# A decoder layer on one core: the cross-attention's masked maxima write their unread sum into the scores' own PSUM bank, not into the residual tile

## The reference

```python
x = _layernorm(x + _L0_attn_ref(x, ...), axis=-1)              # self-attention, 32 heads of 16, no mask
x = _layernorm(x + _L0_xattn_ref(x, ctx_1024, ctx_1024, 0, mask_SxS2_ff0), axis=-1)
x = _layernorm(x + _L0_ffn_ref(x, ...), axis=-1)               # routed, sign weights

# _L0_xattn_ref: 32 query heads, 8 key/value heads (4 query heads share one), head width 16
scores = jnp.einsum('bsgrd,btgd->bgrst', xq, xk) / math.sqrt(HEAD_DIM)
scores = scores + mask                                          # mask is [128 query tokens, 128 context tokens]
probs = jax.nn.softmax(scores.astype(jnp.float32), axis=-1)
out = jnp.einsum('bgrst,btgd->bsgrd', probs, xv)
```

## Time and profile before

| | us |
|---|---|
| median of 3 runs (lowest to highest) | 406.38 (402.18 to 407.63) |
| the profiled execution's own time | 409.41 |
| its span, first to last instruction | 407.6 |
| busy: PE, PEld | 341.6, 244.0 |
| busy: DVE | 267.6 |
| busy: ACT, POOL | 153.7, 113.0 |
| mean granted TensorE clock | 0.864 of full speed |

### The profile page before, as it was taken

How to read it: one execution, slowest core, us unless ns; L and a number is a source line. 1 busy time by engine, 2 the same in 40 slices (tenths; PEclk the granted TensorE clock), 3 DMA queues, 4 the chain that set the end, 5 groups by cost and what they waited for, 6 DMA issues and landing times.

```text
span 407.6 us, 7606 instructions
## 1 busy us (share of the span) xinstructions
PE 341.6 (84%) x2661; PEld 244.0 (60%) x2661; DVE 267.6 (66%) x974; ACT 153.7 (38%) x293; POOL 113.0 (28%) x203
## 2 busy tenths in 40 slices
PE   1693789997889999997999999879899965699563
PEld 1692556795647758975567499666556743444342
DVE  0968653558757648688785497878756777804444
ACT  3852135420144854302375733023755520046220
POOL 3362400131240314433422155421121431000321
PEclk9998568998895999996999999959999976579755
DMA  8948800167570001784510026955000155000001
GB/s 282 374 152 241 183 4 6 56 191 220 145 185 5 12 22 57 206 248 122 167 55 5 0 82 192 260 134 160 5 14 2 44 145 142 4 2 2 0 1 51
DMA packets 26703, 42.59 MB, mean 104 GB/s; under 512 B 8153, under 2 KB 18529, under 8 KB 24361
## 3 DMA queue, kind: packets, MB, share of 16 engines
q1 hardware_dynamic: 26393, 41.58, 36.1%
q10 hardware_dynamic: 272, 0.52, 0.3%
HBM read 29.32 MB, written 12.32 MB: 102 GB/s over the span
## 4 chain that ended last, share of the span: by engine, by line
PE 65%; DVE 20%; issue 5%; DMA 4%; ACT 3%; POOL 2%; SPq 0%; POOLq 0%; DVEq 0%; ACTq 0%
DVE x L778 8%; PE bank_a L883 7%; PE bank_a L884 7%; PE bank_a L885 7%; PE bank_a L962 4%; PE bank_a L932 4%; PE bank_b L1027 4%; PE bank_b L1016 4%; PE bank_a L949 3%; PE bank_b L1017 3%; PE bank_b L1019 3%; PE bank_b L1062 3%; PE bank_b L1063 3%; DVE nma L714 2%; PE bank_b L1004 2%
## 5 line engine op out<-in xcount | busy, mean ns | idle before, releaser
L778 DVE CUSTOM_DVE_ANT_0 x<-bank_b,mraw 128x128 f32<-128x128 f32 x256 | 59.0, 287 | 9.3 <-PE bank_b L1004 2.6
L596 ACT ACTIVATE pb<-bank_b 128x512 f32<-128x512 f32 x64 | 37.6, 600 | 61.7 <-PE bank_b L1019 44.0
L588 ACT ACTIVATE pa<-bank_a 128x512 f32<-128x512 f32 x64 | 37.5, 597 | 26.2 <-PE bank_a L949 13.8
L714 DVE TENSOR_REDUCE nma<-bank_a 128x4 f32<-128x512 f32 x64 | 39.9, 681 | 6.7 <-PE bank_a L932 6.5
L883 PE MATMUL bank_a<-xH,wH 128*128 128x256 f32 x128 | 37.6, 294 | 3.4 <-DVE xL L686 3.4
L1016 PE MATMUL bank_b<-idr,mH 128*128 128x512 f32 x64 | 36.9, 576 | 0.6 <-DVE nmb L778 0.5
L884 PE MATMUL bank_a<-xL,wH 128*128 128x256 f32 x128 | 37.0, 289 | 0.0
L885 PE MATMUL bank_a<-xH,wL 128*128 128x256 f32 x128 | 36.9, 288 | 0.0
L1004 PE MATMUL bank_b<-kx,qx 96*128 96x128 bf16 x256 | 27.0, 252 | 11.5 <-DVE nmb L778 8.9
L932 PE MATMUL bank_a<-ks,qs 96*128 96x128 bf16 x256 | 25.2, 250 | 11.0 <-DMA ks<-scr_k 8.9
L1004 PEld LDWEIGHTS bank_b<-kx,qx 96*128 96x128 bf16 x256 | 18.5, 112 | 20.9 <-DVE nmb L778 12.9
(11 more groups left out here) (160 smaller groups left out, 738.5 us busy)
## 6 DMA issues: line engine op xcount, KB each, us to landing
wraw<-in_L_attn_attn_qkvw_dram SPq DMA_DIRECT2D x3, 1024.0 KB, 8.7
scr_q<-qp SPq DMA_DIRECT2D x8, 384.0 KB, 3.1
qs<-scr_q SPq DMA_DIRECT2D x8, 384.0 KB, 4.5
scr_k<-kp SPq DMA_DIRECT2D x8, 384.0 KB, 4.2
ks<-scr_k SPq DMA_DIRECT2D x8, 384.0 KB, 4.9
scr_x<-xp SPq DMA_DIRECT2D x8, 384.0 KB, 2.7
qx<-scr_x SPq DMA_DIRECT2D x8, 384.0 KB, 4.0
qs<-scr_q SPq DMA_DIRECT2D x8, 256.0 KB, 4.6
```

The costliest lines, as they stand in the source:

```text
L714: dve.tensor_reduce(nma[:, b, 4 * j:4 * j + 4], pa_bank(i, *step)[:].rearrange("p (m t) -> p m t", m=KT), AX.X, ALU.max, negate=True).then ...
L778: last = dve.tensor_tensor_reduce(x2[:, b, r * P:(r + 1) * P], pb_bank(i, *step)[:, r * P:(r + 1) * P], mraw[:], -1.0, -LOWEST, ALU.add, A ...
```

## The change

The elementwise result of the masked maximum now goes back into the block of the bank from which the scores were read. With `x2` no longer written there, the two waits go from the `s` step: the one on DVE's own previous step disappears, and the one on `out_stored` moves to the first step that still writes `x2`, `ot:b,0`.

```diff
@@ B.s, DVE
                     b, g = step[1:]
                     rb.wait_full(dve, i, *step)
 
-                    if g > 0:
-                        rb.wait_emptied(dve, i, "s", b, g - 1)
-                    elif i > 0:
-
-                        dve.wait_ge(out_stored[b], 16 * i)
                     for r in range(4):
                         col = (4 * (g % 2) + r) * KT + g // 2
-                        last = dve.tensor_tensor_reduce(x2[:, b, r * P:(r + 1) * P], pb_bank(i, *step)[:, r * P:(r + 1) * P], mraw[:], -1.0, -LOWEST,
+                        head = pb_bank(i, *step)[:, r * P:(r + 1) * P]
+                        last = dve.tensor_tensor_reduce(head, head, mraw[:], -1.0, -LOWEST,
                                                         ALU.add, ALU.min, nmb[:, b, col:col + 1])
                     last.then_inc(*rb.is_empty(i, *step))
@@ B.ot, DVE
                     rd = rdb[:, 16 * u:16 * u + 16].rearrange("p (r c o) -> p r c o", r=4, o=1)
+                    if i > 0 and u == 0:
+
+                        dve.wait_ge(out_stored[b], 16 * i)
                     dve.reciprocal(rd, v[:, :, :, HD:HD + 1]).then_inc(recip_b[b], 1)
```

## The result

The changed kernel takes 403.2 us (median of 22 runs, 400.1 to 406.8) against 405.65 us for the one before on the same chips (22 runs). The ratio is 0.994, with a 95% interval of 0.991 to 0.997: 2.4 us faster, where 4.5 were forecast. The executions of one kernel spread by up to 2% with the clock they are granted (the kernel before took 402.2 to 408.6 us), and both profiled executions, 409.4 and 406.3 us, are among the slow ones.

The account below looks back on a forecast made before the run. PE was busy 84% and held 65% of the chain; DVE, with 20%, set the pace in some stages. 4.9 us from removed waits less 0.4 for the destination gave 4.5 us less, 401.9 us, range 397 to 410.

Parts of the forecast that it names:

- The price of the wait: Masked maximum across steps: DVE's wait on itself costs 0.44 - 0.21 = 0.23 us; a wait already met is free.
- The bounds: Masked maximum writing to PSUM: from 12 ns quicker to 136 ns slower per instruction, if reads and writes take turns.
- the 33 at which the sum turns: Masked maximum into PSUM: from 4.9 / 150 = 33 ns more per instruction on, the change comes out slower.
- The term put at 0.4 us: PSUM write confirmed later, where the chain leaves DVE: once in each of five stages, at most 0.076 us each.
- The case of a tail no longer overlapped: Rival, chance 0.08: 76 ns write tail no longer beside the next masked maximum, 150 instructions; 6.5 us slower, 412.9.
- The worth of the wait: Waits removed from the chain at the masked maximum, summed over five stages with PE's idle time as cap: 4.9 us.
- the count on the chain: Only waits directly ahead of L778 on the chain count: 24 times, though 41 waits relieve DVE of 9.4 us.
- the cap: PE's idle time limits each stage's gain: 0.06 us in 203 to 215, 1.24 in 284 to 296.
- The DMA's margin: Transposed maxima's DMAs in 341 to 358 us: landing 0.2 to 1.2 us before PE starts, so 1.5 of 1.61 counts.
- a case for the clock: Rival, chance 0.12: shorter waits keep PE's clock up behind 101 us; 8 to 12 us less, about 396.5.
- The moved wait: Wait on the output's store: free at `ot`; left at the score step it could have cost up to 1.0 us.
- the prediction's own signs: Masked maxima 0.21 us apart everywhere means right; 0.29 or 0.35 within a step means a PSUM case.

Follow-up runs that it names:

- all four kernels: Against the kernel before, masked maxima waiting only for the instruction four back: everywhere 0.978, first three groups 0.988, group 0 alone 0.994; or bfloat16 sums in alternating halves, 0.978.
- four kernels alike: Against the kernel before, masked maxima waiting only for the instruction four back: everywhere 0.978, first three groups 0.988, groups 1 and 2 alone 0.992; or bfloat16 sums in alternating halves, 0.978.
- two kernels in which PE's clock was higher: Against the kernel before: unread sum as bfloat16 into two halves of the residual tile in turn, 0.978; wait only for the instruction four back, first three groups, 0.988.
- the kernel with the wait per block everywhere: Kernel before, sum still to the residual tile in SBUF, each masked maximum waiting only for the instruction four back that wrote its block: 396.8 us, ratio 0.978.

## Why the prediction was right or wrong

**The price of the wait**, 0.23 us, and that a met wait is free: right. With the sum left in SBUF the distance across steps is 0.21 us. What the prediction did not see is that the price hangs on the order of the instruction's two waits: 0.12 us if this one is written first.

**The new destination** failed. "I take no change of the start distance, since the read side sets it today": it went from 0.211 to 0.249 us, because the sum and the maximum go to different memories. The bounds held, 12 ns below to 136 above, but the 37 ns in between lie past the 33 at which the sum turns, by the prediction's own figure. The term put at 0.4 us measured 5.4 to 6.4. The case of a tail no longer overlapped, given 0.08, was the nearest to it in size, though not in mechanism: a plain addition into PSUM starts every 0.199 us, as into SBUF. The rule of the Trainium skill that was set aside (Perfetto Trace Analysis, Optimizing Scalar/DVE Operations, 60 and 125 ns) would have given 65 ns; for plain additions the trace shows no such difference, and for the masked maximum 37, which is gone when the maximum goes to PSUM too.

**The worth of the wait** failed in the other direction: the sum gave it 4.9 us and it was 8.8. The failed step is the count on the chain: waits that the chain had not passed over counted as well. The sizes below are from single executions, so what moves by less than a microsecond is sure only where several kernels agree.

- 93 to 101 us: 0.69 predicted for three waits; the masked maxima of this sequence are done 1.40 us sooner in all four kernels, six direct waits. How much of it reached the next sequence is not settled: the stretch is 0.7 to 2.0 us shorter in these, but 0.8 also where nothing was changed in it.
- 203 to 215: 0.35 predicted; 0.19, in four kernels alike, out of 1.1 us that DVE saved. PE had no idle time left to give: the cap was right here, and hard.
- 250 to 266: 1.15 predicted; 1.3 by the masked maxima, 0.8 to 1.0 by the stretch in three kernels, and 3.6 in the one kernel in which the clock there was 0.94 instead of 0.84.
- 284 to 296: 1.24 predicted; 1.50 by the masked maxima in four kernels, 1.0 to 2.0 by the stretch. From the first of them to the last PE's idle time went from 0.65 to 0.06 us, the sign of the cap that the prediction named; the cap itself was a little low.
- 341 to 358: 1.50 predicted; 2.36, all ten direct waits, three of which the chain had not passed over. The DMA's margin held: PE was still released by DVE.
- Stretches put at nothing: 2.7 us in the second in two kernels in which PE's clock was higher, and nothing in the kernel with the wait per block everywhere. In the third it was 1.8 us there, at a clock of 0.94 instead of 0.90, and 0.2 to 0.3 in the others.

In the kernel with the wait per block everywhere the clock thus has a hand in 1.8 + 3.6 of the 10.2 us by which its trace, from the first masked maximum on, is shorter. The prediction had a case for the clock, at 0.12 and in other stretches. How the 8.8 us of the medians divide between DVE and the clock stays open.

The chain of one execution told where the gain was, but not how much.

**The moved wait** is right that it costs nothing at its new place, where no instruction of that line waits for a DMA. Its other half, "could have cost up to 1.0 us", did not come about. In the kernel with the wait per block it stays in its old place, the store is issued at 333.68 us, and the step starts at 336.94, 0.21 behind the instruction before:

```profile
333.68 0.36 SPq L445 DMA_DIRECT2D out_dram<-x  x1
```

**The total**: direction right, 401.9 against 403.2, inside the range, by two terms that were each too small and of opposite sign: 4.9 - 0.4 was forecast, 8.8 - 6.4 measured. That the time came out in the range is luck, and the prediction's own signs tell so, as the distances of 0.25 us are not the 0.21 that it wanted to see. What stays open is the last piece of the 2.4 us: the traces give DVE a gain of 1.0 us from the masked maxima alone, and the stretches of the changed kernel sum to 1.6 from the first masked maximum on. The changed kernel's clock, 0.880 on average over its 22 executions against 0.875 over the 29 of the kernel before, would be worth 0.9 us by the estimate above; that the change raised it is not shown.

## What to carry to other kernels

Where an output is unread, find what it waits for before finding it another place: the hazard was one block four instructions back, and a wait on just that is met and free. Where an instruction has an accumulator output, keep its main output in the memory that the accumulator goes to. And where an instruction has two waits and one of them is on its own engine, write that one first: here it halved its price.

## What the runs showed of the hardware that was not expected

- A masked maximum whose sum and maximum go to different memories costs 37 ns more (0.249 against 0.211 us from start to start, the read of the accumulator 139 ns against 85), in either direction at 128 columns, and 36 ns more with the sum in PSUM at 512. Both in PSUM cost no more than both in SBUF (0.211 us).
- A wait of DVE on its own previous instruction costs 0.12 us where it is the only wait of the instruction or stands first of two in the program, and 0.23 where it stands second, behind the wait for the bank: there it is a piece of its own in the queue, 0.105 us ahead of the instruction.
- PE-bound work of one length took 50.9, 48.2 and 46.8 us at granted clocks of 0.90, 0.97 and 1.00, with the same instructions.
